# Absolute sums of the feed-forward weights in halves, the second half a turn later, ahead of the turned maxima's copy

## The reference

```python
def weight_quant_fake(w):
    scale = 1.0 / jnp.clip(jnp.mean(jnp.abs(w)), 1e-05)
    return jnp.clip(jnp.round(w * scale), -1.0, 1.0) / scale
...
x = x + _L0_xattn_ref(_layernorm(x, axis=-1), ctx_1024, ctx_1024, ...)
x = x + _L0_ffn_ref(_layernorm(x, axis=-1), ..., w1, b1, ..., w2, b2)
x = x + _L1_xattn_ref(_layernorm(x, axis=-1), ctx_1024, ctx_1024, ...)
x = x + _L1_ffn_ref(_layernorm(x, axis=-1), ...)
```

## Time and profile before

| | us |
|---|---|
| median of 3 runs | 385.18 |
| the profiled execution | 385.09 |
| its span, first to last instruction | 383.3 |
| PE (TensorE) busy | 326.1 (85%) |
| DVE (VectorE) busy | 297.4 (78%) |
| ACT (ScalarE) busy | 283.5 (74%) |
| POOL (GpSimd) busy | 235.2 (61%) |

### The profile page before, as it was taken

The page is one execution under the profiler, slowest core; times in us unless marked ns, Lnnn a source line. Parts: engine busy times, 40 slices in busy tenths (PEclk is TensorE's granted clock), DMA queues, the critical chain, the costliest instruction groups (busy, mean ns, idle before and its releaser), DMA issues.

```text
span 383.3 us, 9007 instructions
## 1 busy us (share of the span) xinstructions
PE 326.1 (85%) x2933; PEld 225.1 (59%) x2933; DVE 297.4 (78%) x1014; ACT 283.5 (74%) x594; POOL 235.2 (61%) x278
## 2 busy tenths in 40 slices
PE   7899789999999999756767778678877999999976
PEld 6777566766767665424445545446445666666654
DVE  3899755786988986898998998986446787787884
ACT  5666486677667787837798989887668888888753
POOL 1213543877888897578998898982005546546560
PEclk9999999999999999989899999999999999999999
DMA  7999999999956600000000000000001212212101
GB/s 228 287 286 270 258 226 206 251 215 255 206 109 150 120 1 5 1 0 0 0 2 3 1 0 2 1 2 0 2 15 29 43 43 44 56 43 43 43 16 55
DMA packets 44141, 33.67 MB, mean 88 GB/s; under 512 B 19904, under 2 KB 40256, under 8 KB 43968
## 3 DMA queue, kind: packets, MB, share of 16 engines
q1 hardware_dynamic: 44096, 33.11, 36.1%
HBM read 24.71 MB, written 8.39 MB: 86 GB/s over the span
## 4 chain that ended last, share of the span: by engine, by line
PE 41%; DVE 26%; issue 17%; ACT 8%; DMA 4%; POOL 2%; SPq 1%; DVEq 0%; POOLq 0%; ACTq 0%
PE PS L1751 4%; DVE sm L812 4%; PE PS L1743 4%; PE PS L1409 4%; DMA QT<-scr_k 3%; PE PS L1515 3%; DVE sm L784 3%; PE PS L1481 3%; PE PS L1490 3%; PE PS L1572 3%; PE PS L1713 2%; PE PS L1498 2%; PE PS L1736 2%; DVE negm L673 2%; PE PS L1702 2%
## 5 line engine op out<-in xcount | busy, mean ns | idle before, releaser
L673 DVE TENSOR_REDUCE negm<-PS 128x4 bf16<-128x512 f32 x64 | 41.0, 685 | 13.1 <-PE PS L1490 12.9
L1166 ACT ACTIVATE pT<-PS 128x512 f32<-128x512 f32 x64 | 36.4, 595 | 16.7 <-PE PS L1481 15.9
L499 POOL TENSOR_TENSOR kst<-kst,rows 128x1024 f32<-128x1024 f32 x16 | 38.0, 2372 | 7.9 <-ACT kst L1229 7.9
L1306 ACT ACTIVATE lnT<-PS,Atok 128x128 f32<-128x128 f32 x128 | 36.5, 370 | 2.0 <-DVE lnb L930 0.8
L1621 PE MATMUL PS<-identf,w2f 128*128 128x128 f32 x128 | 17.9, 284 | 18.2 <-ACT w2f L1252 18.2
L516 POOL TENSOR_TENSOR kst<-kst,rows 128x1024 f32<-128x1024 f32 x14 | 33.1, 2367 | 0.0
L538 POOL TENSOR_TENSOR smd<-smd,mhalf 128x1 f32<-128x1 f32 x16 | 9.0, 564 | 37.0 <-DVE smd L998 37.0
L1515 PE MATMUL PS<-pT,vx 128*32 128x128 f32 x512 | 27.3, 285 | 1.8 <-ACT pT L1166 1.8
L544 POOL TENSOR_TENSOR rr<-ms,mhalf 128x8 f32<-128x8 f32 x16 | 26.3, 1646 | 1.9 <-DVE ms L1012 1.9
L1621 PEld LDWEIGHTS PS<-identf,w2f 128*128 128x128 f32 x128 | 14.1, 143 | 22.6 <-ACT w2f L1252 22.4
L930 DVE SCALAR_TENSOR_TENSOR lnb<-PS,lnT 128x512 f32<-128x512 f32 x32 | 20.6, 683 | 8.1 <-PE PS L1713 5.9
(11 more groups left out here) (237 smaller groups left out, 1014.8 us busy)
## 6 DMA issues: line engine op xcount, KB each, us to landing
scr_q<-qpart SPq DMA_DIRECT2D x8, 384.0 KB, 3.5
scr_k<-kpart SPq DMA_DIRECT2D x8, 384.0 KB, 4.6
X<-in_x SPq DMA_DIRECT2D x8, 256.0 KB, 4.9
CTXT<-in_ctxT SPq DMA_DIRECT2D x8, 256.0 KB, 4.7
vx<-in_ctx SPq DMA_DIRECT2D x16, 128.0 KB, 2.7
out<-rest SPq DMA_DIRECT2D x16, 128.0 KB, 1.7
rows<-in_rows SPq DMA_DIRECT2D x1, 1544.0 KB, 14.2
qst<-scr_q SPq DMA_DIRECT2D x8, 192.0 KB, 5.3
```

The source lines that it names most:

```text
L499: gp.tensor_tensor(n2[q.slot], n2[q.slot], ln2g, ALU.mult).then_inc(b_g2, 1)
L673: v.tensor_reduce(negm[f.slot % 2][:, 4 * hg:4 * hg + 4], PS[:, 2 + hg % 2, :].rearrange("p (h k) -> p h k", h=4), AX_X, ALU.max, negate=T ...
L1166: s.activation(pT[:, hg, :], PS[:, hg % 2, :], ACT.Exp, scale=float(DH0) ** -0.5).then_inc(a_e, 1)
L1306: last = s.activation(dT[half][:, cols], PS[:, half, cols], ACT.Exp, scale=1.0, bias=Atok[:, n.b, h:h + 1])
```

## The change

weight_sum now takes a half as well: it sums 1024 of the 2048 columns and writes one of four columns of wabs, which has grown to 128 x 2 x 2. Half 0 of w1 and of w2 stands where the whole sum stood, at the end of ScalarE's turns 5 and 6. Half 1 stands one turn later, in turns 6 and 7, between exponential 2 and the copy to nrows. TensorE's total in turn 7 waits for all four sums and is made by two matmuls that accumulate, one for each half. Nothing else is changed.

```diff
-        wabs = sb("wabs", [128, 2]); wmean = sb("wmean", [128, 2])
+        wabs = sb("wabs", [128, 2, 2]); wmean = sb("wmean", [128, 2])
...
-            def weight_sum(i):
+            def weight_sum(i, half):
                 act.wait_ge(s_w12[i], 16)
-                w, q = ((w1f, w1q), (w2f, w2q))[i]
-                s.activation(q[:].rearrange("p c n -> p (c n)"), w[:].rearrange("p c n -> p (c n)"), ACT.Abs,
-                             accum_out=wabs[:, i:i + 1]).then_inc(s_wsum, 1)
+                cols = slice(half * 1024, half * 1024 + 1024)
+                w, q = [buf[:].rearrange("p c n -> p (c n)")[:, cols] for buf in ((w1f, w1q), (w2f, w2q))[i]]
+                s.activation(q, w, ACT.Abs, accum_out=wabs[:, half, i:i + 1]).then_inc(s_wsum, 1)
...
                 if b:
                     exp(2)
+                if f and f.b in (6, 7):
+                    weight_sum(f.b - 6, 1)
                 if f:
                     act.wait_ge(a_nt, f.b + 1)
...
                 if f and f.b in (5, 6):
-                    weight_sum(f.b - 5)
+                    weight_sum(f.b - 5, 0)
...
-                        pe.wait_ge(s_wsum, 2)
-                        t.matmul(PS[:, 7, 0:2], onesf[:], wabs[:], start=True, stop=True).then_inc(s_wtot, 1)
+                        pe.wait_ge(s_wsum, 4)
+                        for half in range(2):
+                            total = t.matmul(PS[:, 7, 0:2], onesf[:], wabs[:, half, :], start=(half == 0), stop=(half == 1))
+                        total.then_inc(s_wtot, 1)
                         pe.wait_ge(s_wq, 1)
```

## The result

The changed kernel takes 388.76 us (median of 5 runs, 388.23 to 389.13), the kernel before 385.18 us. The ratio is 1.009, with a 95% interval of 1.0076 to 1.0105: slower by 0.9%. Beside the later experiments it took 388.71 us again, ratio 1.0077 (1.0053 to 1.0100). The forecast was 386.7 us with a range to 387.6: the direction was right, the loss of 3.6 us was more than twice the 1.57 us foretold. Three executions far outside are left out of all ratios: two of the kernel before (449.63 and 506.61 us) and one of the later variant f3 (763.0 us).

The account below looks back on a forecast made before the run. The prediction took the chain of waits through TensorE in attention turns 6 and 7 as the bound; 0.18 + 1.19 + 0.20 = +1.57 us on 385.09 gave 386.7 us, range 385.5 to 387.6.

Parts of the forecast that it names:

- The wait of the total: Turn 7: TensorE waits for the last half sum, behind exponential 2; totals start 5.40 us into the turn, +1.19 us.
- The second matmul: Turn 7: the total as two matmuls makes four hardware instructions instead of two, +0.20 us (0.10 to 0.40).
- Half sums of 1.05 us, the freed exponentials: ScalarE: 1.05 us per half; turn 6's exponentials begin 0.85 us earlier, 0.28 us idle goes, no gain at the end.
- Turn 6: w1's second half ahead of nrows delays yT2 and the projection, so turn 7 starts +0.18 us later (0 to 0.62).
- rival C: TensorE's clock falls from turn 7 on through the longer idle time: up to 1.5 us more, 388.2 us, chance 0.04.
- a dip of the clock row near 95 us: Profile sign in TensorE's clock row, named beforehand as one that would show the prediction wrong.
- A: TensorE's delay in turn 7 is absorbed by slack because VectorE sets later turns' starts: 385.3 us, chance 0.13.
- B: Turn 7's last half sum is over by the time yb is ready: only +0.18 + 0.20, 385.5 us, chance 0.05.
- D: Half sum or totals' issue outside its bounds: 386.0 to 386.3 us, chance 0.10, or 387.5 to 388, chance 0.03.

Follow-up runs that it names:

- f3: Kernel before with 35 filler matmuls in the feed-forward stage and the total made ahead of TensorE's wait for yb: 385.23 us, ratio 0.9997.
- e4: Changed kernel with uneven parts, 1536 columns first and 512 in the place of the second half: 387.85 us, ratio 1.0062.
- e8: Changed kernel with the second half sums moved ahead of exponential 2 in ScalarE's order: 385.48 us, ratio 0.9999.
- e1: Changed kernel plus five unused 512-column matmuls ahead of TensorE's wait for the four sums in turn 7: 388.57 us, ratio 1.0077.
- after_again: Changed kernel, unaltered, run a second time beside later experiments: 388.71 us, ratio 1.0077 against the kernel before.
- e3: Changed kernel with only w2 summed in halves; w1 summed whole at the end of turn 5: 387.80 us, ratio 1.0071.
- f1: Changed kernel plus 35 unused filler matmuls in four places of the feed-forward stage: 388.58 us, ratio 1.0069.
- e2: Changed kernel with only w1 summed in halves; w2 summed whole at the end of turn 6: 386.84 us, ratio 1.0038.
- e5: Changed kernel with the total and the means moved one turn later, to turn 8: 387.75 us, ratio 1.0049.
- f2: Changed kernel plus five filler matmuls in turn 7's wait and 35 in the feed-forward stage: 387.52 us, ratio 1.0048.
- e6: Changed kernel with both halves of each matrix summed together at the end of turns 5 and 6: 386.42 us, ratio 1.0023.
- f0: Kernel before plus 35 unused filler matmuls in four places of the feed-forward stage: 384.81 us, ratio 0.9984.

## Why the prediction was wrong

**The wait of the total: right.** Forecast +1.19 us, totals 5.40 us into turn 7; measured 5.37 us, +1.16, released by the accumulator's read. e4 moves the totals by just the part taken from the last sum, and in e8, where that sum is over in time, the wait is gone.

**The second matmul: right.** Forecast +0.20; the transposes follow the start of the totals by 0.83 us instead of 0.64 in the earlier trace rows, +0.19.

**Half sums of 1.05 us, the freed exponentials: right.** 1.05 us each; the 0.28 us idle time of turn 6 is gone. By the page "ScalarE: Activation LUTs" of the Trainium skill, section "What ACT_TABLE_LOAD costs", 1.04 us was estimated; the trace agrees with that length. Its overlap with the next instruction is in the trace as well, but with the accumulator's read, which begins 0.95 us after the half sum (85.12, 86.07). It brought nothing here, since nrows came behind that read and began 1.17 us after the half sum had.

**Turn 6: mechanism right, size wrong.** Forecast +0.18 us, with 0 and 0.62 us as ends. The projection did move to yT2, and turn 7 starts 7.41 us after turn 6. But the term was set off against a landing of 0.44 us that the one profile of before happened to have. Against that one profile the term is 7.41 - 7.24 = +0.17 us, as forecast. Without the landing turn 6 is 6.73 us long, and the term is 7.41 - 6.73 = 0.68 us, above my upper end of 0.62. I had written that the landing "ends the wait at 88.10 whatever TensorE did before" and taken a single execution's transfer for the rule.

**The clock: the step that failed.** The forecast's sum has no term for TensorE's clock; it stands as rival C, with a chance of 0.04 and outside the range. This is the largest missing term; turn 6 is the other. Its price, up to 1.5 us, was nearly right: e1 shows 1.58 us, though 1.33 of it in turn 7 and only 0.25 in turn 8, where the forecast put it. Its chance was wrong, and the sign named for it, a dip of the clock row near 95 us, came. I argued from an almost idle stretch at 185 to 187 us that left the clock up (idle for 1.57 us), and from the matmuls on both sides of turn 7's gap. Against that stood the row of 182 to 183 us at half level, behind a stretch that I read as much worse than turn 7 would be. In turn 7 an idle time of 1.40 us lost the clock in each of the four profiles that had it (after, after_again, e3, f1) and 0.97 us lost it in e4; the nine without such a gap there kept it, with gaps of 0.75 us in turn 6 or 7 among them (e1, e2, e5, f2). The Trainium skill, page "TensorE: Matmul & The Clock Gate", section "Part 4: PE-mode transpose", says that transposes don't count as activity as matmuls do; that rule made a fall likelier, and it fell. Whether the transposes had a part in it no run here tells.

Five of five is not a certainty. At the start of attention every profile, that of before included, has idle times of 1.49, 0.45, 0.20 and 0.80 us within 5.3 us, and behind them the clock fell in seven profiles of the fourteen (after, after_again, e1, e2, e6, e8, f2) and stayed up in seven. In before it stayed up:

```profile
44.23 0.62 PE L1490 MATMUL PS<-kst,qst 96*128 96x128 bf16 x8 [1.49 <-DVE rest L594]
```

```profile
48.00:49.00 1.00, 0.98 (x11) 0.85 (x12) 0.39 (x1) 0.70 (x2) 0.31 (x1) 1.00 1.06 246
```

In after it fell:

```profile
43.60 0.62 PE L1492 MATMUL PS<-kst,qst 96*128 96x128 bf16 x8 [1.49 <-DVE rest L594]
```

```profile
48.00:49.00 1.00, 1.00 (x7) 0.91 (x6) 0.88 (x2) 1.00 (x1) 0.94 (x1) 0.50 1.14 335
```

So the length of an idle time alone doesn't decide, and one trace of a kernel, as the prediction had, can't rule a fall out. How often the changed kernel's turn 7 loses the clock is not known, since only two of its executions were traced.

**The sum.** Between the profiles of before and after the parts are 0.17 us (turn 6), 1.30 us (turns 7 and 8 of e1, 15.10, less 13.80) and 1.58 us (the clock, after's 16.68 less e1's 15.10), together 3.05. Without the clock that is 1.47 us, and 1.57 us were forecast. Against the 20.58 us of f0, without the landing, they are 0.68 + 1.24 + 1.58 = 3.50 us. Both sums are made of the differences they explain; the medians, 3.6 us apart, and f1 against f0 (3.45 us) are the independent measures.

**The other rivals.** A fell: VectorE's read of the total waited with it, and no slack took the delay up. B fell: exponential 2 started 3.60 us into the turn (92.04 - 88.44), as its scores allowed. D was not the case: no size in turn 7 was off.

**Behind turn 9.** The part behind turn 9 takes about 281.4 us in some profiles and 282.5 to 283.2 us in others, and the traces show where. These are VectorE's first two reductions at L812, first in after, then in e2:

```profile
174.21 1.21 DVE L812 TENSOR_REDUCE sm<-kst 128x1 f32<-128x1024 f32 x1
180.87 1.21 DVE L812 TENSOR_REDUCE sm<-kst 128x1 f32<-128x1024 f32 x1
```

```profile
172.02 1.21 DVE L812 TENSOR_REDUCE sm<-kst 128x1 f32<-128x1024 f32 x1
179.87 1.21 DVE L812 TENSOR_REDUCE sm<-kst 128x1 f32<-128x1024 f32 x1
```

They are 6.66 us apart in after, as in before and in f1, and 7.85 us in e2, where the fall of 6.8 us reaches to 174.7. The difference is 1.19 us, just what the eight matmuls shown above take longer there (3.62 instead of 2.43 us). Counted from turn 9, e2, e4 and e6 lose 1.15 to 1.2 us at this one place and e1 0.9; e1 loses another 0.6 us at a fall at 209 us, and e5 1.6 us at one of 6.8 us from 195.5 on. Falls of 3.4 us near 170 and 184 us cost nothing (0.14 us in e5), one that began at 192.5 to 193.4 us cost 0.5 us in f0 and f3. **What stays open** is why the clock stays down for 6.8 us in some executions and 3.4 us in others, and how often a kernel meets the long falls. The medians of e2, e5 and e6 lie 0.5 to 1.3 us above what their three turns say.

## What to carry to other kernels

When a piece of work is cut and its second part moved later, look at what holds the instruction in front of its new place: behind one that waits for the critical engine it cannot start early, and whoever sums up the parts in the same turn waits for all of it; one place further ahead it cost nothing that the time shows (e8). Give an added wait on TensorE two prices, the wait and a fall of the clock behind it; here the second was the larger. Don't give the fall a small chance because one trace has none. And before a cost is covered by a transfer's landing, ask whether that landing is there in every execution.

## What the runs showed of the hardware

An idle time of 0.97 or 1.40 us between busy stretches was followed by 3.4 us at 1.2 GHz in five profiles of five. The fall began only when TensorE was busy again, 1.4 to 2.1 us after its first matmul behind the gap (after: totals from 93.81, fall at 95.4; after_again: 94.03 and 96.1; e4: 92.56 and 94.0). In a longer gap it came inside the gap: in before it began at 167.4, while TensorE stood idle for 4.37 us until 168.09. The same idle time in the same place, 1.49 us at the start of attention, lost the clock in seven executions and kept it in seven. Five matmuls of 512 columns, 1.25 us in all, whose results nobody reads, kept the clock up in turn 7 of e1 and f2. A fall's price depends on where it lies: 1.58 us in turns 7 and 8 of attention, nothing near 170 and 184 us for 3.4 us, 0.9 to 1.2 us near 170 us for 6.8 us.
